# Shifted tokens stored early and sign products on split operands, in an adaLN attention and feed-forward kernel

## What is computed

```python
ga = (2 * (ga >= 0) - 1) * jnp.maximum(jnp.abs(ga), 0.25)      # gb alike
h = _layernorm(x) * (1 + ca) + sa
x = x + ga * (attention(h) @ Wproj.T + bproj)                  # 16 heads of 32
h = _layernorm(x) * (1 + cb) + sb
hidden = fwht(silu(h @ W1.T) * (h @ W3.T))                     # 2048 wide, Walsh-Hadamard
x = x + gb * (hidden @ W2.T)
```

## Time and profile before

| | us |
|---|---|
| median of 3 runs | 3085.48 |
| lowest and highest | 3082.89, 3085.62 |
| the profiled execution | 3086.84 |
| its span | 3084.5 |
| TensorE busy in the span | 3049.4 |

### The profile page before, as it was taken

How to read it: one execution, slowest core, us unless ns; L and a number is a source line. 1 busy time by engine, 2 the same in 40 slices (tenths; PEclk the granted TensorE clock), 3 DMA queues, 4 the chain that set the end, 5 groups by cost and what they waited for, 6 DMA issues and landing times. The chain is left out here.

```text
span 3084.5 us, 41512 instructions
## 1 busy us (share of the span) xinstructions
PE 3049.4 (99%) x15536; PEld 2097.8 (68%) x15536; DVE 1885.7 (61%) x3186; ACT 1529.3 (50%) x2880; POOL 1430.3 (46%) x497
## 2 busy tenths in 40 slices
PE   7999999999999999999999999999999999999999
PEld 5788755555555555555555554788888888888887
DVE  5445988888888888888888874743332323323222
ACT  4333366667766666676666666743222222222221
POOL 2223388888888888888888885000000000000000
PEclk9999999999999999999999999999999999999999
DMA  7665588888888888888888876942211212111111
GB/s 261 198 202 181 157 172 180 182 175 181 180 185 181 177 182 179 183 183 181 181 175 183 182 157 170 309 159 92 72 48 58 69 38 76 45 61 60 45 62 34
DMA packets 149653, 446.91 MB, mean 145 GB/s; under 512 B 26960, under 2 KB 44624, under 8 KB 114256
## 3 DMA queue, kind: packets, MB, share of 16 engines
q0 software_dynamic: 32288, 211.83, 33.5%
q1 hardware_dynamic: 116112, 232.43, 25.4%
q10 hardware_dynamic: 1056, 0.00, 0.0%
HBM read 167.37 MB, written 80.21 MB: 80 GB/s over the span
## 5 line engine op out<-in xcount | busy, mean ns | idle before, releaser
L1268 DVE TENSOR_REDUCE mxp<-pmax 128x1 f32<-128x512 f32 x1968 | 1202.3, 680 | 243.9 <-PE pmax L1046 243.9
L1217 ACT ACTIVATE prob<-pexp 128x512 f32<-128x512 f32 x2023 | 1020.5, 625 | 398.5 <-PE pexp L1095 396.1
L1046 PE MATMUL pmax<-k,q 96*128 96x512 f32 x1968 | 811.2, 412 | 1.1 <-PEq L432 1.1
L1095 PE MATMUL pexp<-q,k 98*128 98x512 f32 x2023 | 803.2, 399 | 0.6 <-ACT prob L1217 0.6
L53 PE MATMUL pproj<-h2f,w 128*128 128x512 f32 x3072 | 717.6, 389 | 0.0
L53 PEld LDWEIGHTS pproj<-h2f,w 128*128 128x128 f32 x3072 | 576.8, 188 | 119.5
L1344 POOL TENSOR_TENSOR gsum<-gsum,prob 128x2048 f32<-128x2048 f32 x127 | 583.5, 4595 | 37.2 <-ACT prob L1217 26.6
L1046 PEld LDWEIGHTS pmax<-k,q 96*128 96x128 f32 x1968 | 373.6, 190 | 280.2 <-DVE mxp L1268 169.7
L1989 POOL TENSOR_TENSOR x2f<-sil,x2f 128x512 f32<-128x512 f32 x1 | 1.3, 1282 | 1085.6 <-DVE sil L1974 1085.6
L1106 PE MATMUL pctx<-prob,v 128*32 128x512 f32 x4096 | 493.4, 598 | 0.0
L1921 DVE TENSOR_TENSOR hid<-sil,pproj 128x512 f32<-128x512 f32 x128 | 88.1, 688 | 630.7 <-PE pproj L53 629.2
(11 more groups left out here) (147 smaller groups left out, 1759.1 us busy)
## 6 DMA issues: line engine op xcount, KB each, us to landing
gsum<-prob POOLq DMA_DIRECT2D x187, 1024.0 KB, 7.4
w<-w_scratch SPq DMA_DIRECT2D x128, 256.0 KB, 2.6
q<-q_scratch SPq DMA_DIRECT2D x96, 256.0 KB, 4.6
k<-k_scratch SPq DMA_DIRECT2D x96, 256.0 KB, 6.2
q_scratch<-obq SPq DMA_DIRECT2D x32, 512.0 KB, 5.3
k_scratch<-obq SPq DMA_DIRECT2D x32, 512.0 KB, 3.7
xin<-in_L_attn_query_dram SPq DMA_DIRECT2D x8, 1024.0 KB, 8.7
v_scratch<-vst SPq DMA_DIRECT2D x8, 1024.0 KB, 5.2
```

Of the source, the lines that this page charges most:

```text
L1046: pe.matmul(pmax[:, bank, :], qst[slot][0:KR, qt * P:(qt + 1) * P], kst[slot][0:KR, kc * TOK:(kc + 1) * TOK], start=True, stop=True).then_ ...
L1095: pe.matmul(score_bank(g, n), kst[slot_of(g)][:, kt * P:(kt + 1) * P], qst[slot_of(g)][:, j * TOK:(j + 1) * TOK], start=True, stop=True).t ...
L1217: act.activation(prob_tile(g, kt)[:, j * TOK:(j + 1) * TOK], score_bank(g, n), ACT.Exp, scale=SCALE).then_inc(exp_done, 1)
L1268: dve.tensor_reduce(mxp[:, par, u // QJ, u % QJ:u % QJ + 1], pmax[:, bank, :], X, ALU.max).then_inc(mx_done, 1)
```

## The change

1. Tokens plus gain times bias are made in the QKV stage, by VectorE, in the `xin` buffers, and stored by SyncE in a new DRAM tensor `shifted`; tokens of tiles 0 and 1 are loaded a second time for this. The projection stage then loads `xres` from there by a plain DMA on SyncE's queue. The copies on ScalarE, the accumulating DMAs on GpSimd and the bias work on VectorE leave that stage.
2. The sign product uses fp32r operands: `signs` (a copy of `had`), and W2 as a high part (written by ScalarE over `w2t`) and a low part (written by VectorE over `full`), so two matmuls take the place of one.

```diff
@@ project_qkv, SyncE @@
+        SHIFTED = (2, 3, 0, 1, 4, 5, 6, 7)
+        SHIFTS = {1: ((2, 8, 1),), 2: ((3, 2, 2), (0, 4, 2), (1, 8, 1)), 3: ((4, 8, 1),), 4: ((5, 2, 1),),
+                  5: ((6, 8, 1),), 6: ((7, 2, 1),)}
                 def load(t):
                     sp.wait_ge(normed, TK * (t - 1))
+                    if t > 3:
+                        sp.wait_ge(x_kept[t % 2], 16 * (t // 2))
                     load_tokens(sp, ins, xin, t).then_inc(x_in[t % 2], 16)
+                def keep_shifted(t):
+                    sp.wait_ge(x_shifted, TK * (SHIFTED.index(t) + 1))
+                    sp.dma_start(scratch["shifted"][t], xin[t % 2][:, :, :].rearrange("p k d -> p (k d)")
+                                 ).then_inc(x_kept[t % 2], 16)
+                def load_again(t):
+                    sp.wait_ge(x_kept[t], 16)
+                    load_tokens(sp, ins, xin, t).then_inc(x_again[t], 16)
                 def store(t):
...
+                        if t == 2 and j == 4:
+                            keep_shifted(3)
+                            load_again(1)
+                        if t == 2 and j == 6:
+                            keep_shifted(0)
                     if t == TILES - 1:
                         return
+                    if t == 0:
+                        send_gains()
+                    if t == 2:
+                        load(4)
+                        keep_shifted(1)
+                    elif t:
+                        keep_shifted(t + 1)
                     sp.wait_ge(out_hi, NJ * (t + 1))
                     store_values(sp, scratch, vst, v_out, t)
                 def load_head(g):
...
+                    sp.wait_ge(x_kept[g], 16 * (ST - g) + 16 * g)
                 for t in range(TILES - 2):
-                    load(t + 2)
+                    if t != 2:
+                        load(t + 2)
+                    if t == 0:
+                        for b in range(B):
+                            sp.dma_start(bias[:, b, :], ins["bproj"].partition_broadcast(P)).then_inc(bias_in, 16)
                     store(t)
+                    if t == 1:
+                        load_again(0)
@@ project_qkv, TensorE @@
-                    pe.wait_ge(keep["had_in"], 16)
+                    pe.wait_ge(signs_set, 1)
                     for i in range(DC):
                         pe.wait_ge(w2_taken, DC * n + i + 1)
-                        pe.matmul(pt[:, i, :], had[:, :], wt[:, i * D:(i + 1) * D], start=True, stop=True).then_inc(w2_mm, 1)
+                        pe.wait_ge(w2_lowered, DC * n + i + 1)
+                        pe.matmul(pt[:, i, :], signs[:, :], w2_high_half[:, i * D:(i + 1) * D], start=True, stop=False)
+                        pe.matmul(pt[:, i, :], signs[:, :], w2_low_half[:, i * D:(i + 1) * D], start=False,
+                                  stop=True).then_inc(w2_mm, 1)
@@ project_qkv, VectorE, in tile(t), after low_result of j @@
+                        if j == FOLD_TURN and t in FOLD_AT:
+                            fold_low(t)
+                        if t == 1 and j == 8:
+                            scale_bias()
+                        for of, since, each in SHIFTS.get(t, ()):
+                            for k in range(TK):
+                                if j == since + k // each:
+                                    shift_tokens(of, k)
+                def shift_tokens(t, k):
+                    if t < 2:
+                        dve.wait_ge(x_again[t], 16)
+                    else:
+                        dve.wait_ge(normed, TK * (t + 1))
+                    dve.tensor_tensor(xin[t % 2][:, k, :], xin[t % 2][:, k, :], bias[:, t // ST, :],
+                                      ALU.add).then_inc(x_shifted, 1)
+                def fold_low(t):
...
+                    for i in range(DC):
+                        dve.wait_ge(w2_taken, DC * n + i + 1)
+                        dve.tensor_tensor(w2_low_half[:, i * D:(i + 1) * D], pt[:, i, :],
+                                          w2_high_half[:, i * D:(i + 1) * D], ALU.subtract).then_inc(w2_lowered, 1)
@@ project_and_feed, SyncE @@
+                def load_x(t):
+                    if t >= 2:
+                        sp.wait_ge(resid, TK * (t - 1))
+                    sp.dma_start(xres[t % 2][:, :, :].rearrange("p k d -> p (k d)"), scratch["shifted"][t]
+                                 ).then_inc(xres_in[t % 2], 16)
                 load_ctx(1)
-                for b in range(B):
-                    sp.dma_start(bias[:, b, :], keep["bproj"].partition_broadcast(P)).then_inc(bias_in, 16)
+                load_x(1)
                 store_last()
...
                     store_x2(t)
+                    if t + 2 < TILES:
+                        load_x(t + 2)
                     if t >= 2:
                         store_h2(t - 2)
@@ project_and_feed, the others @@
-                    fill_residual(t + 2)
-                scale_bias()
-                shift_first()
-                    pool.dma_start(xres[t % 2][:, :, :], ins["x"][b].rearrange("(t k p) d -> t p k d", k=TK, p=P)[s],
-                                   accum_op=ALU.add).then_inc(x_added[t % 2], 16)
```

More of the change, by code:

```diff
@@ L397, in project_qkv @@
         wn = sb("w2n", [P, HID])
+        with ExitStack() as halves:
+            w2_high_half = halves.enter_context(nc.sbuf_tensor("w2_high_half", [P, HID], F32R))
         wt = sb("w2t", [P, HID])
+        signs = sb("signs", [P, P], F32R)
         mark = sb("mark2", [P, 1])
+        bias = sb("bias_rows", [P, B, D])
+        gains_rows = keep["gains"]
+        SHIFTED = (2, 3, 0, 1, 4, 5, 6, 7)
         ps = ctx.enter_context(nc.psum_tensor("ps_qkv", [P, BANKS, TOK], F32))
@@ L409, in project_qkv @@
         gains_out = sem("a_gains_out")
+        gains_in = sem("a_gains_in")
+        bias_in = sem("a_bias_in")
+        bias_scaled = sem("a_bias_scaled")
+        x_again = [sem(f"a_x_again{i}") for i in range(2)]
+        x_shifted = sem("a_x_shifted")
+        x_kept = [sem(f"a_x_kept{i}") for i in range(2)]
         h_hi = sem("a_h_hi")
@@ L595, in fold_take @@
                     n = FOLD_AT.index(t)
-                    if n:
+                    if n == 0:
+                        act.wait_ge(keep["had_in"], 16)
+                        act.activation(signs[:, :], had[:, :], ACT.Copy).then_inc(signs_set, 1)
+                    else:
                         act.wait_ge(w2_out, 16 * n)
@@ L660, in low_parts @@
                     b = t // ST
+                    folded = len([f for f in FOLD_AT if f < t - 1])
+                    if folded:
+                        dve.wait_ge(w2_mm, DC * folded)
                     def whole(c):
@@ L1459, in project_and_feed @@
         resid = sem("c_resid")
-        shifted = sem("c_shifted")
-        filled = sem("c_filled")
-        x_added = [sem(f"c_x_added{i}") for i in range(2)]
-        bias_scaled = sem("c_bias_scaled")
-        bias_in = sem("c_bias_in")
         chain = sem("c_chain")
@@ L1799, in high_part @@
                     act.activation(h2[:, b, HI, :, :], raw(h2[:, b, LO, :, :]), ACT.Copy).then_inc(h_hi, 1)
-                def fill_residual(t):
-                    if t == 1:
-                        act.wait_ge(bias_scaled, 1)
-                    else:
-                        act.wait_ge(resid, TK * (t - 1))
-                    for k in range(TK):
-                        last = act.activation(xres[t % 2][:, k, :], bias[:, t // ST, :], ACT.Copy)
-                    last.then_inc(filled, 1)
                 def weights_high(m):
@@ L1824, in _ @@
                 ctx_high(1)
-                fill_residual(1)
                 for t in range(TILES - 2):
@@ L1856, in ctx_low @@
                                           ALU.subtract).then_inc(c_lo, 1)
-                def scale_bias():
-                    dve.wait_ge(bias_in, 16 * B)
-                    dve.tensor_tensor(bias[:, :, :], bias[:, :, :], gains[:, :, :], ALU.mult).then_inc(bias_scaled, 1)
-                    dve.wait_ge(bias_scaled, 1)
-                def shift_first():
-                    dve.wait_ge(xres_in[0], 16)
-                    for k in range(TK):
-                        dve.tensor_tensor(xres[0][:, k, :], xres[0][:, k, :], bias[:, 0, :], ALU.add).then_inc(shifted, 1)
                 def residual(t):
@@ L1980, in _ @@
             def _(pool):
-                for t in range(1, TILES):
-                    b, s = where(t)
-                    pool.wait_ge(filled, t)
-                    pool.dma_start(xres[t % 2][:, :, :], ins["x"][b].rearrange("(t k p) d -> t p k d", k=TK, p=P)[s],
-                                   accum_op=ALU.add).then_inc(x_added[t % 2], 16)
                 pool.wait_ge(x_in, 16 * TILES)
```

42 lines of the change are left out of this document (24 added, 18 removed).

## The result

The changed kernel takes 3087.64 us (median of 22 runs, 3081.58 to 3097.59); the kernel before takes 3084.01 in the runs beside it. The ratio is 1.0015, with an interval of 1.0009 to 1.0021: a loss of 0.15%, small but clear of the interval, where 3073 was forecast. The profiled execution took 3089.05 us, its span is 3087.2.

What follows compares the result with a forecast made beforehand. It took TensorE, busy 3049.4 of 3084.5 us, as the bound. QKV -3.7, projection start -4.5, period -1.9 and end -2.7 sum to -12.8, giving 3073 us against the median, range 3067 to 3080.

Steps and rivals of the forecast that it cites:

- Sign products, -6.4: QKV stage: fp32r pairs replace plain float32 products, saving TensorE 1.6 us in each of 4 folds, -6.4 us.
- What this uncovers: +0.7, +0.7, +0.8: QKV stage: shorter folds leave GpSimd later as TensorE sees it; +0.7 us in tile 5, +0.7 in tile 1, +0.8 in tile 3.
- Shifts in the QKV stage: +0.5 for late tokens in tile 3: Tile 4's tokens, queued behind stores and a reload, land 1 to 2 us late: +0.5 us, between 0 and 2.
- VectorE's additions elsewhere, `fold_low`, signs, bias: nothing: QKV stage: VectorE's other additions, `fold_low`, the signs copy and bias loads stay hidden, costing nothing.
- Projection, the start, -4.5: `project(1)` follows `project(0)` without a wait, 2.9 us, and 1.6 us of clock loss goes: -4.5 us.
- The period, -1.9: Projection: without `fill_residual` ScalarE is ready sooner, so long periods shorten by 0.9 us each; two count, -1.9 us.
- the third long one: The last of three long projection periods, worth 0.9 us, which the forecast counted with the stage's end.
- The end, -2.7: Before `turn_rows(0)`: `load_h` lands 2.7 us sooner as DMA is relieved, -2.7 us; bounds 2.6 later to 7.6 sooner.
- My rival (`load_x(7)` goes ahead of `load_h`): Projection's end gives nothing or loses because `load_x(7)` precedes `load_h` in one queue: 3078 us, 14%.
- the QKV stage giving nothing: VectorE's additions meet butterflies, or the pair of sign products comes no cheaper than the one: 3077 us, 14%.
- The one for ctx landing late: Projection: `load_x(t + 2)` ahead in SyncE's queue makes ctx late, stalling each of five periods: 3098 us, 4%.
- The sum: QKV stage -3.7, projection start -4.5, period -1.9 and end -2.7 us: -12.8 us in all, 3073 against the median.

Runs made afterwards that it cites:

- experiment 1: The kernel before with only the split sign products, nothing of the tokens moved: 3083.95 us against 3082.78, ratio 1.0008.
- experiment 3: The changed kernel with tile 0's store ahead of the second load of tile 1 in SyncE's queue: 3085.24 us, ratio 1.001 to the kernel before.
- Experiment 5: The changed kernel with the scaled W2 block written to `full`, so GpSimd's next butterfly needn't await its store: 3086.13 us, ratio 1.0011 to the kernel before.
- experiment 8: The changed kernel with tile 0's store before tile 1's reload, `load_x(7)` behind `load_h(0, 0)` and the butterfly ahead: 3072.43 us, ratio 0.997 to the kernel before.
- experiment 4: The changed kernel with `load_x(7)` moved behind `load_h(0, 0)` on SyncE's queue: 3082.07 us, ratio 0.9999 to the kernel before.
- experiment 7: The kernel before with the projection's tokens loaded plainly, gain times bias left out, nothing added to the QKV stage: 3078.55 us, ratio 0.9988.
- experiment 9: The changed kernel with two queue reorderings, the butterfly ahead, and GpSimd's butterflies held until VectorE's statistics are written: 3065.9 us, ratio 0.9947 to the kernel before.
- experiment 6: The kernel before with the split sign products and the butterfly ahead, no token moves: 3080.41 us, ratio 0.9993.
- experiment 10: Both kernels unchanged, profiled again: the kernel before 3083.14 us against 3083.65, ratio 0.9998; the changed kernel 3087.74 in one execution.

## Why the prediction was wrong

Step by step, in the order of the text on record.

- **Sign products, -6.4.** Right: 1.64 for each fold.
- **What this uncovers: +0.7, +0.7, +0.8.** The places were right and each term too small: +1.8 (tile 5), +1.7 (tile 1), and in tile 3 2.5 in experiment 1, 3.25 in experiment 3. I priced them by GpSimd's delay of 0.7 us, since I had its store and butterfly 0.9 sooner. In tile 0 the store was issued sooner but landed later, and the butterfly started no sooner on the stage's clock; so all of TensorE's 1.6 us came up against it, and it lay over more of line 669's four (8.06 and 9.09 us for the four, 6.40 before), one more held in tile 1 of the changed kernel and all four in experiment 3. The Trainium skill (SBUF — State Buffer, "Who interferes with whom") says that a VectorE instruction with two SBUF inputs and a GpSimd instruction that reads SBUF contend, one being blocked for the whole of the other, and by that rule I had worked out up to 2.6 us each for tiles 1 and 3. The measured 1.7 lies between that and my 0.7, the 2.5 is near it and the 3.25 above it; I had cited the rule and not let it decide. The same section says that only VectorE's two-input and two-port forms contend with GpSimd, and that `tensor_scalar` can be such a two-port form. Experiment 5 agrees with it: line 326 has two SBUF inputs, line 320 is a `tensor_scalar` from SBUF to SBUF, and both were held, while the `reciprocal` between them took its usual 0.18 us; that line 320 ran in a two-port form no trace shows.
- **Shifts in the QKV stage: +0.5 for late tokens in tile 3, between 0 and 2.** This is the step that failed most: 7.1 us of stall and 2.5 of clock. The mechanism was named, and the ladder of queue and landings was laid out; the rungs were put at 6, 10 and 8.7 us, with an issue on time. Measured rungs are 8.1, 13.6 and 8.0, and the landing is 5.3 us late on the stage's clock (164.0 for 157, less the stage's later start of 1.7). I had put the landing 1 to 2 us after the need, and by the measured need it would have been 1.8: with the 5.3 that is the stall. I had then taken the median low. A chain of three landings that stands on the path should have had the sum of their upper ends as its upper end.
- **VectorE's additions elsewhere, `fold_low`, signs, bias: nothing.** Right: in the changed kernel's traces no wait is put down to them. In experiment 8 tile 3 waits 0.6 longer than tiles 1 and 5, and there `shift_tokens(1, 3)` stands ahead of `fold_scale`; that was not tested.
- **Projection, the start, -4.5.** Right to 0.1 against the first trace (-4.57), but part of that is luck: 1.6 of it was clock that this stage, as it was before, lost in one of four traces: against the second trace of the kernel before the step is worth 2.9.
- **The period, -1.9.** Right, with the third long one -2.85 (-3.1 between the second traces).
- **The end, -2.7.** Wrong in sign: the wait grew by 1.8 between the first traces and also between the second (4.0 to 5.8). As the forecast counts it, with the third long period (-0.95) included, that is +0.8. The load landed in 1.6 us less, but it was issued 3.3 later relative to `project(7)`, and I had counted on relief without that. In all six traces of this end that I compared (both kernels twice, experiments 4 and 7) `turn_rows(0)` starts 4.75 us after the load has landed, so the landing alone sets it. My rival (`load_x(7)` goes ahead of `load_h`) had 14%, and experiment 4 shows that it is what happens: 4.9 us of landing and 4.6 of the stage for moving one load. That experiment's lead is only 0.3 us longer, so the 2.16 us of its issue are not the cause.
- **The rivals.** The end giving nothing, and the QKV stage giving nothing, both came true together, and the second by more than its price, by a mechanism I held at +0.5. The one for ctx landing late did not come, though its sign did: ScalarE's waits for `cin` in this stage grew from 15.2 us to 30.7, and they cost TensorE nothing.
- **The sum.** -12.8 forecast; -7.3 (projection) + 6.4 (QKV) = -0.9 measured between the first traces in the parts that were edited; the other 3.6 us of the difference in span are start and attention. Between the second traces it is -3.9 + 7.2 = +3.3. In the first pair the projection's start, periods and end wait (-4.6, -2.85 and +1.8) come to -5.6; the other 1.7 of the 7.3 is clock that the first trace of the kernel before lost behind that wait, and that no term of the forecast held.

What stays open is attention. In both traces of the kernel before no matmul in it ran at the 1.2 GHz level. In nine of the eleven traces with an edit (the changed kernel twice among them) there are one or two stretches of 3.4 us at that level, mostly near its end, in code that no edit touched. Attention is 1.3 to 2.4 us longer there with one stretch and 2.9 to 3.7 with two than in the mean of the two traces of the kernel before; experiments 4 and 9 have none. That is too few traces to say whether an edit's shift in time brings them on or chance does. The start varies likewise, 32.2 to 34.3, between traces of one kernel.

## What to carry to other kernels

When a step goes through one in-order queue as store, wait, load, wait, write down every landing with its upper end and add them; here a ladder of three landed 5.3 us later than forecast, with its queue's packets at 82% of the engines' time, and the cure was the order. When TensorE gets faster, look at what VectorE and GpSimd then do beside each other: here their meeting took back 5.2 of the 6.6 us. In the traces the faster products gave 0.7 us by themselves and 3.7 with the butterfly moved ahead (0.1 and 3.1 against the second trace, and neither is told from nothing by the times), and a wait that keeps it off two tiny operations gave 5.1 more. And put a large load that isn't urgent behind the one that is.

## What the runs showed that I had not expected

- Two VectorE operations on 128 x 4 numbers, 0.17 and 0.16 us by themselves, took 1.10 to 1.71 and 1.93 to 1.97 us beside GpSimd's butterfly in tiles 1, 3 and 5 of experiments 5, 6 and 8, and 1.2 to 1.8 us of each of these tiles hung on them in experiments 6 and 8; experiment 9 shows it.
- The issue of `load_x` on SyncE took 0.42 us at 1972.84 in the changed kernel and 2.16 at 1985.48, and four row loads behind it 3.66, where that queue's packets took 98.1% of the 16 engines' time between 1985 and 2008 us. What sets it is not shown: between 1968 and 1973 us, at the short one, the engines' share was 0.89. In experiment 4 the store that came in its place took 1.93.

```profile
q1 hardware_dynamic: 2004, 8.38, 98.1%
```

- The stall of 2.6 to 2.9 us before `project(1)` cost clock in the first trace of the kernel before (12.80 for the 48 matmuls behind it) and none in the three other traces of that stage as it was (11.19 in experiment 10, 11.20 in 1, 11.22 in 6), with the same instructions and the same wait. A term of clock read from one trace needs a second trace.
